# Cross-attention with a mixture-of-experts FFN on one core: when ScalarE and GpSimd split queries and single-key products, and how much of the single key's tile GpSimd splits

## The chip, the cores and the metric

The kernel runs on one core of a Trainium2 chip. The engines are TensorE (PE in the profile, with PEld for its weight loads), VectorE (DVE), ScalarE (ACT), GpSimd (POOL) and SyncE (SP), which issues the DMAs. The metric is the device time of one execution in microseconds, as the median over runs; a time is called faster or slower here when it moves by more than 0.3%.

## The reference

For each of 16 batch elements, 56 query rows of width 256 attend to 1500 context rows. The first 257 context rows (the image part) and the other 1243 (the text part) have keys, values and a softmax of their own; the two results are added.

```python
q = rms_norm(x @ q_w + q_b, nq_s).reshape(B, S, H, D)        # H = 16 heads, D = 128
k_txt = rms_norm(txt_ctx @ k_w + k_b, nkt_s).reshape(B, -1, H, D)
v_txt = (txt_ctx @ v_w + v_b).reshape(B, -1, H, D)
out_txt = sdpa(q, k_txt, v_txt)
k_img = rms_norm(img_ctx @ ki_w + ki_b, nki_s).reshape(B, -1, H, D)
v_img = (img_ctx @ vi_w + vi_b).reshape(B, -1, H, D)
out_img = sdpa(q, k_img, v_img)
out = (out_txt + out_img).reshape(B, S, INNER) @ o_w + o_b
```

A layer norm and a small mixture of 32 experts follow, with residual sums. All is in float32.

## The kernel before

The key projection is absorbed into the queries, so that attention works on the 256 columns of the context itself. The program first makes these absorbed queries (project), then runs attention over the 16 batch elements (attend), then the output projection and the experts. The change lies in attend alone.

**Tiles and steps.** The context of one batch element is cut into 13 tiles: tiles 0 to 2 are the image part, tiles 3 to 12 the text part. Tile 2 (LONE) holds one single key, since 257 = 2 x 128 + 1. All 16 heads times 56 queries are 896 columns, taken in two halves of 448. One half of one tile is a unit, so a batch element is 26 units, and every engine runs through 26 steps written out by hand. The batch loop is `batches`: its first and last passes are apart, with 14 loop passes between. Each engine executes its own list of instructions in order and waits on semaphores.

**High and low parts.** A float32 product is made of three fp32r matmuls (`three`, L1162 to L1164) of a high part and a low part of each operand. ScalarE makes a high part by a copy into fp32r (`copy`, L1314), and GpSimd or VectorE subtracts it from the original, which gives the low part.

**What each engine does for tile t** (column 0 to 255 of a tile's row of `stage` are the context with features on the partitions, columns 256 to 511 the natural layout):

- ScalarE: `prepare` (c_high, L1314, 512 columns); `exponentials` of each unit (L1341 and L1343), which at a tile's first half wait for key_rms of the tile; in some steps `split_u` (u_high, the high part of the next queries) and `split_lone` (the tile x_high in the trace, the high part of the single key's products).
- GpSimd, odd step: `split_tile` (c_low, L1636) and `twice` (c_twice, L1649; for LONE also lone_row, L1645) of a tile three steps or so ahead. After it, at the steps in LONE_LOW, `split_lone` (L1686, the low part of the single key's products, which the trace also names x_high). Even step: `key_root` (key_rms, L1630), and then one of scale_u (L1655), split_u (u_low, L1680) or scale_o (L1698).
- VectorE: `norm` (junk and key_ms, L1449), which reads c_twice; `split_probs` (p_low, L1424), `add` (L1477 or L1480) and `seed` (L1435), which writes the next unit's starting values to PSUM; at a few steps `split_sum` (p_sum_high L1488 and p_sum_low L1424, both from SBUF to SBUF).
- TensorE: the scores of a unit, the norm's products (L1169, L1171) at even steps, and the average of the unit two steps back (L1162 to L1164 with p_high), which waits for p_low.

`key_root` of a tile waits for `norm` of that tile, and `norm` waits for `twice` of that tile. For GpSimd the order is set by this part of `body`, and for ScalarE by the tuples tested at the end of its own:

```python
if step % 2 == 0:
    key_root(*ahead(it, step // 2 + 1))
else:
    split_tile(*ahead(it, step // 2 + PREP))
    twice(*ahead(it, step // 2 + PREP))
...
if has_next and step in LONE_LOW:
    split_lone(it + 1, LONE_LOW.index(step))
```

Of the kernel before, what the change touches and what calls it, by code (L numbers as in the profile page):

```python
# [23 lines left out]
F32 = mybir.dt.float32  # L24
F32R = mybir.dt.float32r
ACT = mybir.ActivationFunctionType
ALU = mybir.AluOpType
# [3 lines left out]
B, S, DIM = 16, 56, 256  # L31
# [14 lines left out]
LONE = IMG_TILES - 1  # L46
# [14 lines left out]
STAGE_RING, CTX_RING, TWICE_RING, U_RING = 3, 4, 2, 2  # L61
# [21 lines left out]
def slot(t, ring):  # L83

    return t % ring if t < TILES - 1 else ring
# [95 lines left out]
def build(nc, xT_in, ctx_in, lone_in, qw_in, kw_in, kwb_in, vw_in, small_in, router_in, bias_in, ffn_in, out):  # L181
    ctx = ExitStack()
    with ctx:
# [15 lines left out]
        with attn:  # L199
# [19 lines left out]
            with proj:  # L219

                x_high = sb("x_high", [P, NC, N], F32R, proj)
                x_low = sb("x_low", [P, NC, N], F32R, proj)
                bias_high = sb("bias_high", [P, BIAS_FLAT], F32R, proj)
                bias_low = sb("bias_low", [P, BIAS_FLAT], F32R, proj)
                square_w = sb("square_w", [P, H, 1 + 2 * H], F32R, proj)
                begun = prologue(nc, xT_in, kwb_in, small_in, psum, xT, ident, ones, minus_half, zeros, small, key_scale,
                                 bias_high, bias_low, v_bias, x_high, x_low, gram_high, gram_low, lin_rows, lin_pick,
                                 ones_r, square_w)
                by_head = [x[:, 0:2 * H * H].rearrange("p (h k) -> p h k", h=H) for x in (bias_high, bias_low)]
                spent = attend(nc, ctx_in, lone_in, qw_in, kw_in, psum, ident, minus_half, zeros, small, key_scale, *by_head,  # L230
                               x_high, x_low, square_w, gram_high, gram_low, lin_rows, lin_pick, ones_r, u_dram,
                               beta_dram, o_dram, u_stage, u_raw, q_rms_wide, is_safe, u_stored, begun)
# [568 lines left out]
def attend(nc, ctx_in, lone_in, qw_in, kw_in, psum, ident, minus_half, zeros, small, key_scale, bias_high, bias_low, x_high,  # L801
# [4 lines left out]
    with ctx:  # L806
# [3 lines left out]
        def sem(n):  # L810
            spent.append(nc.alloc_semaphore(name=n))
            return spent[-1]
# [4 lines left out]
        stage = sb("stage", [P, STAGE_RING + 1, 2 * DIM])  # L817
        c_high = sb("c_high", [P, CTX_RING + 1, 2 * DIM], F32R)
        c_low = sb("c_low", [P, CTX_RING + 1, 2 * DIM], F32R)
# [12 lines left out]
        ctx_high, ctx_low, stage_used = sem("ctx_high"), sem("ctx_low"), sem("stage_used")  # L832
# [64 lines left out]

        O = 0
        IMAGE, TEXT = 0, 1
        TEXT_SPLIT, IMAGE_SPLIT = (1, 3), (10, 12)  # L900
        LONE_TERMS, LONE_HIGH, LONE_LOW = (12, 14), (14, 16), (17, 19)
        TEXT_SUM_SPLIT, TEXT_SUMS, TEXT_RECIP = (1, 2), (3, 5), 10
        IMAGE_SUM_SPLIT, IMAGE_SUMS, IMAGE_RECIP = (7, 8), (9, 11), 16

# [718 lines left out]
        def _(gp):  # L1623
# [7 lines left out]
                    .then_inc(key_norm, 1)  # L1631

            def split_tile(it, t):
                k, st = slot(t, CTX_RING), slot(t, STAGE_RING)
                gp.wait_ge(ctx_high, TILES * it + t + 1)
                nc.gpsimd.tensor_tensor(c_low[:, k, :], stage[:, st, :], c_high[:, k, :].bitcast(F32), ALU.subtract)\  # L1636
                    .then_inc(ctx_low, 1)

            def twice(it, t):
                k, st, T = slot(t, CTX_RING), slot(t, STAGE_RING), TILES * it + t  # L1640
# [60 lines left out]
            def body(it, has_prev, has_next):  # L1701
                if not has_prev:
                    scale_first(TEXT, 0)
                for step in range(UNITS):
# [5 lines that stand above are left out]
                    if step == 0 and has_prev:  # L1710
                        scale_u(it, TEXT, 1)
                    if step == 0 and not has_prev:
                        scale_first(TEXT, 1)
                    if not has_prev and step in (1, 2):
                        split_lone(it, step - 1)
                    if has_next and step in LONE_LOW:
                        split_lone(it + 1, LONE_LOW.index(step))
                    if step in (2, 4):
                        split_u(it, TEXT, (step - 2) // 2)
                    if has_next and step in (8, 10):  # L1720
                        scale_u(it + 1, IMAGE, (step - 8) // 2)
                    if has_next and step in (12, 14):
                        split_u(it + 1, IMAGE, (step - 12) // 2)
                    if has_prev and step in (16, 18):
                        scale_o(it - 1, TEXT, (step - 16) // 2)
                    if step in (20, 22):
                        scale_o(it, IMAGE, (step - 20) // 2)
                    if has_next and step == 24:
                        scale_u(it + 1, TEXT, 0)
# [609 lines left out]
```

## Time and profile before

| | before |
|---|---|
| median of 3 runs | 1903.29 us (1898.18 to 1903.45) |
| profiled execution, its time | 1903.73 us |
| profiled execution, its span | 1902.0 us |
| mean granted TensorE clock | 0.971 |
| PE / DVE / ACT / POOL busy | 91% / 73% / 52% / 63% |

The span runs from the first to the last instruction of the one execution that was profiled. Attention lies from about 239 us to 1432 us in it. Busy shares are averages over the whole span; a matmul's row shows its whole duration, of which a part overlaps the next one.

### The profile page before, as it was taken

How to read it: one execution, taken by the hardware profiler on the slowest of the kernel's cores; microseconds unless marked ns; L12 is line 12 of the kernel's file. 1: busy time of each engine (PE TensorE's matmuls, PEld its weight loads, DVE VectorE, ACT ScalarE, POOL GpSimd, SP SyncE). 2: the span in 40 equal slices, each digit the busy share in tenths (PEclk: the TensorE clock that was granted, in tenths of full speed). 3: DMA queues.
4: the chain of work that ended last, by engine and by line, in shares of the span. 5: the costliest groups of instructions: out<-in, count | busy, mean ns of one | idle time of the engine just before them, and what ended most of it. 6: DMA issues, size and time to landing. Idle time of an engine off the chain costs nothing. (4 is left out here: it accounts for less than half of the span.)

```text
span 1902.0 us, 30825 instructions
## 1 busy us (share of the span) xinstructions
PE 1733.7 (91%) x8731; PEld 1541.6 (81%) x8731; DVE 1397.3 (73%) x2577; ACT 985.9 (52%) x1657; POOL 1204.3 (63%) x1053
## 2 busy tenths in 40 slices
PE   7899889999999999999999999999992998699998
PEld 6677778888889889888888898898891886588887
DVE  4444587887887887978878878879772664577776
ACT  3455455565555555655655565556552563244443
POOL 1333588878878888788788798798862231133332
PEclk9999899999999999999999999999996999799999
DMA  3366554566556465554565564564436782133332
GB/s 110 127 239 232 175 164 104 114 123 137 115 118 131 108 117 123 121 120 113 128 132 118 120 134 103 116 128 123 95 92 203 249 267 88 66 109 118 114 115 74
DMA packets 417365, 251.20 MB, mean 132 GB/s; under 512 B 350272, under 2 KB 368832, under 8 KB 415520
## 3 DMA queue, kind: packets, MB, share of 16 engines
q1 hardware_dynamic: 417312, 250.55, 51.5%
q8 instruction: 26, 0.43, 0.1%
q14 instruction: 27, 0.22, 0.0%
HBM read 187.71 MB, written 60.10 MB: 130 GB/s over the span
## 5 line engine op out<-in xcount | busy, mean ns | idle before, releaser
L1341 ACT ACTIVATE p_high<-psum,key_rms 128x448 fp32r<-128x448 f32 x384 | 244.8, 638 | 397.1 <-PE psum L1164 396.9
L1162 PE MATMUL psum<-p_high,c_high 128*128 128x448 f32 (+1 forms) x768 | 287.8, 375 | 48.2 <-DVE p_low L1424 48.2
L1424 DVE TENSOR_TENSOR p_low<-psum,p_high 128x448 fp32r<-128x448 f32 x384 | 236.3, 615 | 96.6 <-ACT psum L1343 95.7
L1162 PE MATMUL psum<-u_high,c_high 128*128 128x448 f32 x768 | 285.9, 372 | 20.2 <-DVE psum L1435 14.1
L1163 PE MATMUL psum<-u_low,c_high 128*128 128x448 f32 x768 | 282.9, 368 | 0.0
L1164 PE MATMUL psum<-u_high,c_low 128*128 128x448 f32 x768 | 281.8, 367 | 0.0
L1164 PE MATMUL psum<-p_high,c_low 128*128 128x448 f32 (+1 forms) x768 | 281.4, 366 | 0.0
L1163 PE MATMUL psum<-p_low,c_high 128*128 128x448 f32 (+1 forms) x768 | 281.0, 366 | 0.0
L1636 POOL TENSOR_TENSOR c_low<-stage,c_high 128x512 fp32r<-128x512 f32 x208 | 274.7, 1321 | 0.0
L1435 DVE COPY psum<-beta_wide 128x448 f32<-128x448 f32 x416 | 259.4, 627 | 20.3 <-DMA beta_wide<-absorbed_biases 4.5
L1630 POOL TENSOR_TENSOR key_rms<-key_ms,minus_half 128x1 f32<-128x1 f32 x209 | 119.4, 571 | 188.4 <-DVE key_ms L1449 183.4
L1343 ACT ACTIVATE psum<-psum,key_rms 128x448 f32<-128x448 f32 x384 | 232.5, 606 | 0.0
L1162 PEld LDWEIGHTS psum<-p_high,c_high 128*128 128x128 f32 (+1 forms) x768 | 144.0, 188 | 72.9 <-DVE p_low L1424 62.2
L1480 DVE TENSOR_TENSOR p_sum<-psum,p_sum 128x448 f32<-128x448 f32 (+1 forms) x320 | 196.2, 613 | 0.0
L1162 PEld LDWEIGHTS psum<-u_high,c_high 128*128 128x128 f32 x768 | 144.9, 189 | 44.8 <-DVE psum L1435 20.7
L2043 POOL TENSOR_TENSOR scaled_gate<-gated,p_wide 128x448 f32<-128x448 f32 x64 | 83.7, 1308 | 154.0 <-ACT gated L2144 150.5
L1649 POOL TENSOR_TENSOR c_twice<-stage,c_low 128x256 f32<-128x256 f32 x208 | 169.9, 817 | 16.4 <-POOL c_low L1636 2.4
L1449 DVE CUSTOM_DVE_ANT_0 junk<-psum,c_twice 128x257 bf16<-128x257 f32 x208 | 88.6, 426 | 92.2 <-POOL c_twice L1649 90.3
L1164 PEld LDWEIGHTS psum<-u_high,c_low 128*128 128x128 f32 x768 | 145.2, 189 | 12.7
L1163 PEld LDWEIGHTS psum<-u_low,c_high 128*128 128x128 f32 x768 | 145.2, 189 | 10.9
L1164 PEld LDWEIGHTS psum<-p_high,c_low 128*128 128x128 f32 (+1 forms) x768 | 144.1, 188 | 12.1
L1163 PEld LDWEIGHTS psum<-p_low,c_high 128*128 128x128 f32 (+1 forms) x768 | 144.3, 188 | 8.6
(245 smaller groups left out, 4077.9 us busy)
## 6 DMA issues: line engine op xcount, KB each, us to landing
stage<-in_ctx SPq DMA_DIRECT2D x210, 256.0 KB, 2.8
averages<-o_raw SPq DMA_DIRECT2D x64, 448.0 KB, 5.2
o_stage<-averages SPq DMA_DIRECT2D x32, 896.0 KB, 5.4
u_raw<-absorbed_queries SPq DMA_DIRECT2D x60, 448.0 KB, 5.5
absorbed_queries<-u_stage SPq DMA_DIRECT2D x14, 1792.0 KB, 6.8
beta_wide<-absorbed_biases SPq DMA_DIRECT2D x32, 448.0 KB, 5.3
recip_wide<-reciprocals SPq DMA_DIRECT2D x32, 448.0 KB, 4.1
p_wide<-probs_by_expert SPq DMA_DIRECT2D x32, 448.0 KB, 3.6
```

The costliest lines, as they stand in the source:

```text
L1162: nc.tensor.matmul(out, high, rhigh, start=start, stop=False, **kw)
L1163: nc.tensor.matmul(out, high, rlow, start=False, stop=False, **kw)
L1164: return nc.tensor.matmul(out, low, rhigh, start=False, stop=stop, **kw)
L1341: nc.scalar.activation(p_high[:, probs_slot(u), :], src, ACT.Exp, scale=key_rms[:, t:t + 1])
L1343: nc.scalar.activation(out, src, ACT.Exp, scale=key_rms[:, t:t + 1]).then_inc(exp_done, 1)
L1424: return nc.vector.tensor_tensor(out, a, b, ALU.subtract)
L1435: nc.vector.tensor_copy(psum[:, bank_of(u), 0:HALF], beta_wide[:, s, cols_of(half)])\
L1449: nc.vector.tensor_tensor_reduce(out=junk[:, :], in0=psum[:, GRAM, 0:DIM + 1], in1=c_twice[:, slot(t, TWICE_RING), :], scale=1.0 / INNER, ...
L1480: added = nc.vector.tensor_tensor(total, part, total, ALU.add)
L1630: nc.gpsimd.tensor_tensor(key_rms[:, t:t + 1], key_ms[:, t:t + 1], minus_half[:, 0:1], ALU.pow)\
L1636: nc.gpsimd.tensor_tensor(c_low[:, k, :], stage[:, st, :], c_high[:, k, :].bitcast(F32), ALU.subtract)\
L1649: nc.gpsimd.tensor_tensor(c_twice[:, slot(t, TWICE_RING), 0:DIM], stage[:, st, nat], c_low[:, k, nat].bitcast(F32), ALU.add).then_inc(stag ...
```

## The change

Three tuples of step numbers change, and `split_tile` takes a column range. The high parts of the next batch element's image queries go from steps 10 and 12 to 11 and 13 on ScalarE; the high parts of the single key's products go from steps 14 and 16 to 15 and 17; their low parts on GpSimd go from steps 17 and 19 to 18 and 20. For the single key's tile GpSimd subtracts only columns 256 to 511, the half that anything reads later.

```diff
-        TEXT_SPLIT, IMAGE_SPLIT = (1, 3), (10, 12)
-        LONE_TERMS, LONE_HIGH, LONE_LOW = (12, 14), (14, 16), (17, 19)
+        TEXT_SPLIT, IMAGE_SPLIT = (1, 3), (11, 13)
+        LONE_TERMS, LONE_HIGH, LONE_LOW = (12, 14), (15, 17), (18, 20)
...
             def split_tile(it, t):
-                k, st = slot(t, CTX_RING), slot(t, STAGE_RING)
+                k, st, cols = slot(t, CTX_RING), slot(t, STAGE_RING), slice(DIM if t == LONE else 0, 2 * DIM)
                 gp.wait_ge(ctx_high, TILES * it + t + 1)
-                nc.gpsimd.tensor_tensor(c_low[:, k, :], stage[:, st, :], c_high[:, k, :].bitcast(F32), ALU.subtract)\
-                    .then_inc(ctx_low, 1)
+                nc.gpsimd.tensor_tensor(c_low[:, k, cols], stage[:, st, cols], c_high[:, k, cols].bitcast(F32),
+                                        ALU.subtract).then_inc(ctx_low, 1)
```

GpSimd in the loop over the batch elements, steps 17 to 20, before (x_high is the low part of the single key's products, o_raw the scaling of finished averages):

```order
L1649 TENSOR_TENSOR c_twice<-stage,c_low 128x256
L1685 ISA
L1686 TENSOR_TENSOR x_high<-lone_terms,x_high 128x448
L1629 REGISTER_ALU
L1630 TENSOR_TENSOR key_rms<-key_ms,minus_half 128x1
L1695 REGISTER_ALU
L1698 TENSOR_TENSOR o_raw<-o_raw,recip_wide 128x2x448
L1636 TENSOR_TENSOR c_low<-stage,c_high 128x512
```

The same place of the changed kernel:

```order
L1649 TENSOR_TENSOR c_twice<-stage,c_low 128x256
L1629 REGISTER_ALU
L1630 TENSOR_TENSOR key_rms<-key_ms,minus_half 128x1
L1685 ISA
L1686 TENSOR_TENSOR x_high<-lone_terms,x_high 128x448
L1695 REGISTER_ALU
L1698 TENSOR_TENSOR o_raw<-o_raw,recip_wide 128x2x448
L1636 TENSOR_TENSOR c_low<-stage,c_high 128x512
```

The subtract of the single key's products stood between c_twice and key_rms and now stands between key_rms and o_raw; the same happens once more, at steps 19 and 20.

GpSimd at the start of a batch element in the loop, steps 0 to 3, of the changed kernel:

```order
L1630 TENSOR_TENSOR key_rms<-key_ms,minus_half 128x1
L1655 TENSOR_TENSOR u_raw<-u_raw,rms_batch 128x2x448
L1636 TENSOR_TENSOR c_low<-stage,c_high 128x256
L1645 TENSOR_TENSOR lone_row<-stage,zeros 128x2
L1649 TENSOR_TENSOR c_twice<-stage,c_low 128x256
L1630 TENSOR_TENSOR key_rms<-key_ms,minus_half 128x1
```

Here no row has moved; the c_low of the single key's tile had 128x512 and has 128x256.

## Rows read from the trace of the kernel before

**Rows 1.** Waits of PE and of POOL: engine, line, waited for, us in total, times, longest

```profile
PE psum L1162 <- DVE p_low L1424: 48.2, 48, 2.7
...
POOL key_rms L1630 <- DVE key_ms L1449: 183.4, 178, 2.9
```

**Rows 2.** Busy time by stretch of one batch element: window, length, then PE, PEld, DVE, ACT, POOL

```profile
612.10:645.10 33.00, 29.13 (x149) 25.24 (x148) 31.78 (x57) 21.10 (x37) 25.06 (x23) 1.00 0.58 128
645.10:689.30 44.20, 44.20 (x234) 41.06 (x234) 32.55 (x69) 24.79 (x44) 40.14 (x35) 1.00 0.60 121
```

**Rows 3.** Timeline of PE: start us, us, what [idle before it <- releaser]

```profile
620.93 0.47 PE L1162 MATMUL psum<-p_high,c_high 128*128 128x448 f32 x1 [1.43 <-DVE p_low L1424]
...
638.51 0.47 PE L1162 MATMUL psum<-p_high,c_high 128*128 128x448 f32 x1 [1.27 <-DVE p_low L1424]
...
677.52 0.37 PE L1162 MATMUL psum<-p_high,c_high 128*128 128x448 f32 x1
```

**Rows 4.** Timeline of DVE, steps 1 to 3 of a batch element, then later ones

```profile
612.08 0.62 DVE L1424 TENSOR_TENSOR p_low<-psum,p_high 128x448 fp32r<-128x448 f32 x1 [2.17 <-ACT psum L1343]
...
613.80 0.38 DVE L1488 CAST p_sum_high<-p_sum 128x448 fp32r<-128x448 f32 x1
614.22 1.19 DVE L1424 TENSOR_TENSOR p_sum_low<-p_sum,p_sum_high 128x448 fp32r<-128x448 f32 x1
615.33 0.42 DVE L1449 CUSTOM_DVE_ANT_0 junk<-psum,c_twice 128x257 bf16<-128x257 f32 x1
...
617.39 1.33 DVE L1488 CAST p_sum_high<-p_sum 128x448 fp32r<-128x448 f32 x1
...
645.11 0.42 DVE L1449 CUSTOM_DVE_ANT_0 junk<-psum,c_twice 128x257 bf16<-128x257 f32 x1
...
673.38 0.43 DVE L1449 CUSTOM_DVE_ANT_0 junk<-psum,c_twice 128x257 bf16<-128x257 f32 x1 [1.15 <-POOL c_twice L1649]
...
673.73 0.62 DVE L1424 TENSOR_TENSOR p_low<-psum,p_high 128x448 fp32r<-128x448 f32 x1
...
689.77 0.42 DVE L1449 CUSTOM_DVE_ANT_0 junk<-psum,c_twice 128x257 bf16<-128x257 f32 x1
```

**Rows 5.** Timeline of POOL, the same batch element

```profile
612.58 1.29 POOL L1636 TENSOR_TENSOR c_low<-stage,c_high 128x512 fp32r<-128x512 f32 x1
...
614.19 0.73 POOL L1649 TENSOR_TENSOR c_twice<-stage,c_low 128x256 f32<-128x256 f32 x1
...
618.42 1.43 POOL L1636 TENSOR_TENSOR c_low<-stage,c_high 128x512 fp32r<-128x512 f32 x1
...
660.93 0.74 POOL L1649 TENSOR_TENSOR c_twice<-stage,c_low 128x256 f32<-128x256 f32 x1
661.62 1.17 POOL L1686 TENSOR_TENSOR x_high<-lone_terms,x_high 128x448 fp32r<-128x448 f32 x1
662.73 0.56 POOL L1630 TENSOR_TENSOR key_rms<-key_ms,minus_half 128x1 f32<-128x1 f32 x1
663.25 2.14 POOL L1698 TENSOR_TENSOR o_raw<-o_raw,recip_wide 128x896 f32<-128x896 f32 x1
...
677.88 0.74 POOL L1649 TENSOR_TENSOR c_twice<-stage,c_low 128x256 f32<-128x256 f32 x1
679.17 0.55 POOL L1630 TENSOR_TENSOR key_rms<-key_ms,minus_half 128x1 f32<-128x1 f32 x1 [0.55 <-DVE key_ms L1449]
```

**Rows 6.** Timeline of ACT around the moved copies

```profile
636.08 0.96 ACT L1314 ACTIVATE u_high<-u_raw 128x896 fp32r<-128x896 f32 x1
636.94 0.61 ACT L1341 ACTIVATE p_high<-psum,key_rms 128x448 fp32r<-128x448 f32 x1
```

**Rows 7.** POOL and DVE where the second batch element begins

```profile
315.94 0.74 POOL L1649 TENSOR_TENSOR c_twice<-stage,c_low 128x256 f32<-128x256 f32 x1
...
314.36 0.63 DVE L1424 TENSOR_TENSOR p_low<-psum,p_high 128x448 fp32r<-128x448 f32 x1 [2.71 <-ACT psum L1343]
...
317.50 0.42 DVE L1449 CUSTOM_DVE_ANT_0 junk<-psum,c_twice 128x257 bf16<-128x257 f32 x1
```

## The prediction

> **What bounds the kernel now.** I read the waits first. In the attention stage TensorE waits mostly for VectorE's p_low, 48.2 us in 48 waits, and GpSimd waits 178 times for VectorE's norm, 183.4 us in all, although both are below 75% busy in the page [rows 1]. Then I read the timelines of one batch element, which repeats: the norm at 615.33 has its like at 689.77, so the period is 74.44 us [rows 4]. Busy time in two stretches of that period shows two regimes. From 612.1 to 645.1 VectorE is busy for 31.78 of 33.00 us and TensorE for only 29.13; from 645.1 to 689.3 TensorE is busy throughout, but GpSimd has 40.14 of 44.20 [rows 2].
>
> The missing 4 us of GpSimd in the second stretch is the thing to see. After c_twice of a tile, VectorE computes the norm, and only then can GpSimd go on with key_rms: 677.88 to 679.17 is 1.29 us, in which GpSimd sits idle for 0.55 [rows 5]. In turn VectorE waits for c_twice at 673.38, for 1.15 us [rows 4]. So in the second stretch GpSimd runs a closed chain, its own work plus a 0.55 us round trip for each tile, and nothing of TensorE enters it. It arrives at the c_twice of the single key's tile (614.19, and one period later 688.63), whose norm VectorE needs at once (615.33). From that norm VectorE is busy without a stop worth naming to the norm at 645.11, where GpSimd's chain starts again [rows 2, 4, 5]. I take this loop, VectorE for 30 us and GpSimd for 44 us, as what sets 74.44. TensorE's stalls, 1.43 us at 620.93 and 1.27 at 638.51 [rows 3], are where it waits for the loop.
>
> A second path reaches the norm at 615.33. VectorE starts p_low at 612.08 after ScalarE and so after TensorE [rows 4]. To the cast at 613.80 it takes 1.72, to p_sum_low 0.42, and p_sum_low itself needs about 0.49: it ran to 615.41, and c_twice ended at 614.92. That is 2.63 us against the 3.25 taken (612.08 to 615.33). The 0.62 us more is GpSimd's doing, so the TensorE path is only 0.62 us short of the loop.
>
> **The subtracts of the single key's products, steps 17 and 19 to 18 and 20.** Before, the subtract at 661.62 filled the round trip: key_rms at 662.73 shows no idle time, and from c_twice at 660.93 to o_raw at 663.25 it is 2.32 us [rows 5]. After, c_twice to key_rms is the bare 1.29, key_rms to the next instruction 0.52 (662.73 to 663.25), and the subtract 1.11 (661.62 to 662.73): 2.92 us. That is 0.60 more, twice in a batch element: GpSimd is 1.20 us later from step 20 on. Behind it stand all its later rows, the loads of stage that SyncE issues upon c_twice, and VectorE's norms. VectorE has been waiting at each norm, so it passes the delay on: p_low at 673.73 moves to 674.9 and ends at 675.5, still before TensorE needs it at 677.52 [rows 3, 4]. The loads are three tiles ahead, some 17 us (three thirteenths of 74.44), and hide it.
>
> **The shorter subtract of the single key's tile.** Now 1.29 us for 512 columns; the 256 columns of c_twice take 0.73 [rows 5]. I take 0.73, a saving of 0.56. Net, c_twice at 688.63 comes 0.64 later: 689.27 to 690.00. Without any other interference the norm starts at 690.03 in place of 689.77, 0.26 us later.
>
> **The interference.** The cast at 617.39 took 1.33 us where the one at 613.80 took 0.38; it ended 0.30 us after GpSimd's next instruction began at 618.42, and that one, of the same form as at 612.58, took 1.43 instead of 1.29 [rows 4, 5]. So a cast or a subtract of VectorE from SBUF to SBUF and an instruction of GpSimd exclude each other. In the changed kernel the cast comes at 613.80 + 74.44 = 688.24, and GpSimd's c_low at 687.02 + 1.20 = 688.22: a tie.
> - c_low first: the cast waits to 688.95 and ends at 689.26. Then p_sum_low (0.49) and c_twice (0.73) follow one another, in whichever order, to about 690.52; the norm starts at 690.55, 0.78 later than before.
> - The cast first: it is through at 688.55, c_low is pushed by 0.14 to end at 689.09, p_sum_low takes until 689.58, c_twice until about 690.25, and the norm starts at 690.28, 0.51 later.
>
> The middle, 0.65 us, is my value. The row at 617.39 speaks for the second (a waiting VectorE gets in before GpSimd's next), the 0.02 us of the tie for the first.
>
> The Trainium skill ("SBUF — State Buffer", Who interferes with whom) gives the rule behind this: VectorE's second port pair is GpSimd's only one, and whoever issues first has it for the whole instruction. The trace agrees in the 1.33 us cast; by that rule taken strictly, c_low would win the tie and the time would be 14 x 0.78 - 0.5 = 10.4 us over before, 1914.1, instead of the middle.
>
> **The moved copies of ScalarE.** I cost them at nothing. u_high at 636.08 delays the exponentials behind it, at 636.94, by up to 0.86 us [rows 6], but VectorE, which is to read them, is behind there: it is busy for 31.78 of 33.00 us. At most the 1.2 us that it idles in that stretch could be a gain, 15 x 1.2 = 18 us faster. Were ScalarE later than VectorE, the new place could cost as much. The copies' readers, GpSimd's subtracts, stand one step or more behind them; a late one would add to the 1.20.
>
> **The sum.** The delay counts at each start of a batch element in the loop, and the norm, the instructions after it and TensorE behind them shift alike, since all of them follow the loop. The first passage differs. There c_twice was already early, at 315.94, 1.58 us after VectorE's p_low at 314.36 (2.11 in the steady case, 612.08 to 614.19), and the norm was no earlier than 3.14 us after p_low, because the cast met c_twice [rows 7]. Batch element 0 lacks two scalings of GpSimd, so it can take the moved subtracts, and the shorter c_low then puts c_twice before the cast: up to 3.14 - 2.63 = 0.5 us gained, once. The sum is 14 x 0.65 - 0.5 = 8.6 us on the profiled execution's own 1903.73, so 1912.3; the median of the runs lies 0.44 below that execution, which gives **1912**.
>
> **The rivals.** What a measurement can tell from no change is about 0.3%, 5.7 us.
> - No interference remains at the norm: 14 x 0.26 - 0.5 = 3.1 us, about 1907. For it: c_twice moves away from its old meeting with p_sum_low. Against: the cast meets c_low instead.
> - The lateness is absorbed, because GpSimd waits somewhere for TensorE after all. Then only the shorter subtract counts, and the first passage shows what it is worth: 3.14 for 3.25, 0.11 us. 15 x 0.11 = 1.7 us faster, about 1902. Against: in the second stretch each idle time before key_rms is the bare 0.55.
> - Faster: GpSimd comes so early that VectorE meets none of its instructions before the norm, and the path by way of TensorE decides: 15 x 0.62 = 9 us, about 1894. It needs c_twice to end before the cast at 688.24, over 1.1 us earlier than now; the shorter subtract gives half of this, and the move takes more than that away. A gain of the moved copies of ScalarE would end there too.
> - Slower than forecast: the whole 1.20 us is paid, since a meeting eats the saving, or another one is lost downstream: 14 x 1.2 = 17 us, about 1920.
>
> **Chances.** Forecast (0.5 to 0.8 us a passage, 1910 to 1915) 0.60; no interference 0.16; absorbed 0.10; faster 0.07; the whole delay 0.07. Faster by over 0.3% is 0.07, slower 0.67, the two in between 0.26. The range goes from 1901, which takes in the absorbed case, to 1917.
>
> **What the changed profile would show.** A batch element of 75.1 us in place of 74.44; 0.55 us of idle time before the key_rms of steps 18 and 20, with the subtract behind it; o_raw 0.60 and then 1.20 us later against TensorE; c_low of the single key's tile at about 0.73 us; TensorE's stall that stood at 620.93 longer by as much as the period. If the period stays at 74.4 with those delays in place, the loop is not what I took it for. If the cast before the norm is short and p_sum_low too, the interference was mis-sized.

## The result and the profile after

The changed kernel takes 1910.02 us (median of 6 runs, 1909.05 to 1915.24) against 1901.92 us before (6 runs): the ratio is 1.005, with a 95% interval of 1.0034 to 1.0066. (The ratios here are worked out from all runs and are not the quotient of two medians, which would be 1.0043.) It is 8.1 us slower by the medians, at 1910 us for the forecast 1912; 8.6 us were forecast.

The page of the profiled execution, first part:

```profile
span 1907.3 us, 30825 instructions
## 1 busy us (share of the span) xinstructions
PE 1734.7 (91%) x8731; PEld 1538.3 (81%) x8731; DVE 1392.0 (73%) x2577; ACT 988.4 (52%) x1657; POOL 1197.2 (63%) x1053
```

POOL does 7 us less work than the 1204.3 us that its page had before, and the kernel is longer. The waits of the changed kernel (engine, line, waited for: us in total, times, longest):

```profile
PE psum L1162 <- DVE p_low L1424: 45.8, 48, 2.7
...
PE psum L1162 <- DVE psum L1435: 22.7, 29, 1.2
...
POOL key_rms L1630 <- DVE key_ms L1449: 199.9, 207, 2.9
```

Against [rows 1], GpSimd waits 29 times more for VectorE's norm and 16.5 us longer in all. 29 waits of 0.55 us would be 16 us. TensorE's wait for p_low is a little shorter; its wait for psum L1435, VectorE's seed, was 14.1 us in 15 waits before and is 22.7 in 29. The loss shows there, and not where I had put it: by the prediction the stall that stood at 620.93 in [rows 3] was to grow with the batch element, and in the changed kernel it is 1.32 us instead of 1.43, the same distance behind the first scores.

```profile
619.74 0.47 PE L1162 MATMUL psum<-p_high,c_high 128*128 128x448 f32 x1 [1.32 <-DVE p_low L1424]
```

The timeline of POOL in the changed kernel, around the first moved subtract and at the single key's tile:

```profile
659.70 0.74 POOL L1649 TENSOR_TENSOR c_twice<-stage,c_low 128x256 f32<-128x256 f32 x1
660.99 0.55 POOL L1630 TENSOR_TENSOR key_rms<-key_ms,minus_half 128x1 f32<-128x1 f32 x1 [0.55 <-DVE key_ms L1449]
661.51 1.15 POOL L1686 TENSOR_TENSOR x_high<-lone_terms,x_high 128x448 fp32r<-128x448 f32 x1
662.62 2.13 POOL L1698 TENSOR_TENSOR o_raw<-o_raw,recip_wide 128x896 f32<-128x896 f32 x1
...
686.91 0.74 POOL L1636 TENSOR_TENSOR c_low<-stage,c_high 128x256 fp32r<-128x256 f32 x1
687.81 0.19 POOL L1645 TENSOR_TENSOR lone_row<-stage,zeros 128x2 f32<-128x2 f32 x1 [0.16 <-POOL c_low L1636]
687.96 0.96 POOL L1649 TENSOR_TENSOR c_twice<-stage,c_low 128x256 f32<-128x256 f32 x1
```

From c_twice to o_raw it is 2.92 us, where [rows 5] have 2.32: the 0.55 us wait before key_rms stands bare, and the subtract comes behind it. The c_low of the single key's tile takes 0.74 us instead of 1.29. The loads of stage cost nothing more: during attention ScalarE waits for one of them twice, 6.5 us in all before and 6.4 after.

The timeline of VectorE in the changed kernel, from step 22 to the start of the next batch element:

```profile
673.32 0.43 DVE L1449 CUSTOM_DVE_ANT_0 junk<-psum,c_twice 128x257 bf16<-128x257 f32 x1 [2.30 <-POOL c_twice L1649]
...
678.57 0.43 DVE L1449 CUSTOM_DVE_ANT_0 junk<-psum,c_twice 128x257 bf16<-128x257 f32 x1 [1.27 <-POOL c_twice L1649]
678.92 0.08 DVE L1449 DVE_READ_ACCUMULATOR2_ANT key_ms<- 128x1 f32 x1
678.92 0.62 DVE L1424 TENSOR_TENSOR p_low<-psum,p_high 128x448 fp32r<-128x448 f32 x1
679.46 0.61 DVE L1480 TENSOR_TENSOR p_sum<-psum,p_sum 91x448 f32<-91x448 f32 x1
680.10 0.63 DVE L1435 COPY psum<-beta_wide 128x448 f32<-128x448 f32 x1
...
686.21 0.62 DVE L1424 TENSOR_TENSOR p_low<-psum,p_high 128x448 fp32r<-128x448 f32 x1 [1.98 <-ACT psum L1343]
...
687.94 0.39 DVE L1488 CAST p_sum_high<-p_sum 128x448 fp32r<-128x448 f32 x1
688.36 1.04 DVE L1424 TENSOR_TENSOR p_sum_low<-p_sum,p_sum_high 128x448 fp32r<-128x448 f32 x1
689.32 0.42 DVE L1449 CUSTOM_DVE_ANT_0 junk<-psum,c_twice 128x257 bf16<-128x257 f32 x1
```

VectorE waits 2.30 us for c_twice where [rows 4] have 1.15. The norm at 678.57 comes late too, and behind it stand the p_low of the last unit but one and then a copy, at 680.10. This copy is the seed of the next batch element's first unit. TensorE's timeline there:

```profile
680.78 0.48 PE L1162 MATMUL psum<-u_high,c_high 128*128 128x448 f32 x1 [0.62 <-DVE psum L1435]
```

It waits for this seed before the first scores of the batch element. In the kernel before, the same seed and the same matmul were these rows of DVE and PE, 0.39 us apart (680.18 + 0.63 to 681.20):

```profile
680.18 0.63 DVE L1435 COPY psum<-beta_wide 128x448 f32<-128x448 f32 x1
...
681.20 0.37 PE L1162 MATMUL psum<-u_high,c_high 128*128 128x448 f32 x1
```

The norms of the single key's tile (VectorE, changed kernel) give the length of a batch element: 689.32 less 614.12 is 75.20 us, where [rows 4] have 74.44.

```profile
614.12 0.42 DVE L1449 CUSTOM_DVE_ANT_0 junk<-psum,c_twice 128x257 bf16<-128x257 f32 x1
```

### The profile page after: what moved, and what is told of

The parts are those of the page before. It is cut to its first block and busy times, and to the rows that moved or that the text cites. A ratio compares the mean times of both kernels' runs of the same rounds, so it can differ in the third digit from the quotient of the medians.

```text
span 1907.3 us, 30825 instructions
## 1 busy us (share of the span) xinstructions
PE 1734.7 (91%) x8731; PEld 1538.3 (81%) x8731; DVE 1392.0 (73%) x2577; ACT 988.4 (52%) x1657; POOL 1197.2 (63%) x1053
## 5 line engine op out<-in xcount | busy, mean ns | idle before, releaser
L1162 PE MATMUL psum<-u_high,c_high 128*128 128x448 f32 x768 | 287.0, 374 | 28.8 <-DVE psum L1435 22.7
L1435 DVE COPY psum<-beta_wide 128x448 f32<-128x448 f32 x416 | 259.3, 627 | 20.4 <-DMA beta_wide<-absorbed_biases 4.5
L1636 POOL TENSOR_TENSOR c_low<-stage,c_high 128x512 fp32r<-128x512 f32 (+1 forms) x208 | 264.8, 1273 | 0.0
```

What stands on the lines that cost most here:

```text
L1162: nc.tensor.matmul(out, high, rhigh, start=start, stop=False, **kw)
L1435: nc.vector.tensor_copy(psum[:, bank_of(u), 0:HALF], beta_wide[:, s, cols_of(half)])\
L1636: nc.gpsimd.tensor_tensor(c_low[:, k, cols], stage[:, st, cols], c_high[:, k, cols].bitcast(F32), ALU.subtract).then_inc(ctx_low, 1)
```

## The experiments

The table has three numbers of each kernel's timeline besides its time. *Stall* is what TensorE loses at the first scores of a batch element: the time from the start of the matmul before them to the start of their first one, less the 0.20 us that it is without a stall. *Norm* is how long after VectorE's first p_low of a batch element the norm of the single key's tile starts (in [rows 4] 612.08 and 615.33). *Element* is the mean length of batch elements 2 to 15 (the first is 1), from first scores to first scores. Stall and norm are those of most batch elements.

| kernel | ratio to before, 95% interval | stall | norm | element |
|---|---|---|---|---|
| before | | 0 | 3.25 | 74.46 |
| changed | 1.005 (1.0034 to 1.0066) | 0.77 | 3.11 | 75.18 |
| e1, GpSimd's move only | 1.0115 (1.0099 to 1.0131) | 0.83 | 3.59 | 75.95 |
| e2, narrower c_low only | 0.9981 (0.9972 to 0.9990) | 0 | 3.11 | 74.32 |
| e3, ScalarE's moves only | 1.0000 (0.9991 to 1.0009) | 0 | 3.25 | 74.52 |
| e4, all but GpSimd's move | 0.9983 (0.9973 to 0.9993) | 0 | 3.11 | 74.29 |
| e5, steps 19 and 21 | 0.9977 (0.9966 to 0.9987) | 0 | 3.02 | 74.25 |
| e6, steps 17 and 20 | 0.9998 (0.9990 to 1.0007) | 0.19 | 3.11 | 74.61 |
| e10, norm behind the seed | 1.0069 (1.0054 to 1.0084) | 0 | 4.16 | 75.42 |
| e9, second half at step 3 | 0.9941 (0.9923 to 0.9959) | 0 | 2.69 | 73.91 |

One sum runs through the table. A batch element is 74.46, plus the stall and some 0.1 us with which the matmuls start again behind it, plus the norm's distance less 3.25. For e6 this is 74.46 + 0.19 + 0.09 - 0.14 = 74.60, for e10 74.46 + 0.91 = 75.37, for e9 74.46 - 0.56 = 73.90. For e1 it is 75.7, and 0.2 us are left over (last section). The mean of e3 holds two elements near its start of 74.96 and 74.87 us, whose cause is open; its others are 74.41 to 74.48.

### e1 to e4: the parts by themselves

e1 is the kernel before with this edit alone:

```diff
-        LONE_TERMS, LONE_HIGH, LONE_LOW = (12, 14), (14, 16), (17, 19)
+        LONE_TERMS, LONE_HIGH, LONE_LOW = (12, 14), (14, 16), (18, 20)
```

> Only the low parts of the single key's products move, steps 17 and 19 to 18 and 20; c_low of the single key's tile keeps its 512 columns, ScalarE keeps its order. Theory 1 (the move makes GpSimd 1.20 us late; VectorE's norm at step 24 passes this to the seed of the next batch element's first unit, and TensorE stalls for about 0.77 us at its first scores; behind this the whole-width c_low also makes the norm of the single key's tile later): the stall of 0.7 to 0.8 is there, the norm comes 3.3 to 3.6 us after VectorE's p_low instead of 3.11, a batch element is 75.4 to 75.8 us, 13 to 18 us over before, ratio 1.007 to 1.010. Theory 2 (only the seed's stall counts): 75.2 us as in the changed kernel, ratio 1.005. Theory 3 (the moved copies of ScalarE are what costs): no stall, 74.4 us, ratio 1.000.

It is 1.0115, slower than any theory had it: seven of its batch elements took 76.2 us, for a reason told in the last section; the other steady ones took 75.7, within the range of theory 1. The stall is there, and the norm comes at 3.59, as theory 1 said. That the seed's stall alone counts (theory 2) is refuted. The move, taken by itself, costs more than the whole change.

e2 is the kernel before with the new `split_tile` only:

```diff
-                k, st = slot(t, CTX_RING), slot(t, STAGE_RING)
+                k, st, cols = slot(t, CTX_RING), slot(t, STAGE_RING), slice(DIM if t == LONE else 0, 2 * DIM)
...
```

> Only the narrower c_low of the single key's tile; all steps as before. Theories 1 and 2: no stall at a batch element's first scores; c_twice starts 0.56 us earlier against VectorE's p_low and meets the cast, as it did at the second batch element of the kernel before, so the norm comes 3.14 us after p_low instead of 3.25: 0.11 us a batch element, 1.7 us faster, ratio 0.999. If the loop by way of GpSimd alone set the period, the gain would be up to 0.56 x 15 = 8 us, ratio 0.996. Theory 3: ratio 1.000 or just under.

Ratio 0.9981, a little below the 0.999 expected; from the first scores of the first batch element to those of the last it is 2.4 us shorter than before, for the 1.7 expected. The timelines of DVE and POOL in e2:

```profile
606.96 0.62 DVE L1424 TENSOR_TENSOR p_low<-psum,p_high 128x448 fp32r<-128x448 f32 x1 [2.17 <-ACT psum L1343]
...
608.68 0.81 DVE L1488 CAST p_sum_high<-p_sum 128x448 fp32r<-128x448 f32 x1
609.53 0.63 DVE L1424 TENSOR_TENSOR p_sum_low<-p_sum,p_sum_high 128x448 fp32r<-128x448 f32 x1
610.07 0.42 DVE L1449 CUSTOM_DVE_ANT_0 junk<-psum,c_twice 128x257 bf16<-128x257 f32 x1
...
608.51 0.74 POOL L1649 TENSOR_TENSOR c_twice<-stage,c_low 128x256 f32<-128x256 f32 x1
```

c_twice runs from 608.51 to 609.25, and the cast, started at 608.68, takes 0.81 us instead of 0.38. The 0.56 us that GpSimd saves come down to 0.14: c_twice no longer holds up p_sum_low, it holds up the cast. This is the meeting that [rows 7] show.

e3 is the kernel before with ScalarE's moves, two tuples of two steps each:

```diff
-        TEXT_SPLIT, IMAGE_SPLIT = (1, 3), (10, 12)
-        LONE_TERMS, LONE_HIGH, LONE_LOW = (12, 14), (14, 16), (17, 19)
+        TEXT_SPLIT, IMAGE_SPLIT = (1, 3), (11, 13)
+        LONE_TERMS, LONE_HIGH, LONE_LOW = (12, 14), (15, 17), (17, 19)
```

> Only ScalarE's copies move (image queries to steps 11 and 13, high parts of the single key's products to 15 and 17); GpSimd as before. Theories 1 and 2: no effect, batch element 74.4 us, ratio 0.999 to 1.001. Theory 3: ratio 1.005, a batch element of 75.2 us.

Ratio 1.0000: nothing, and theory 3 falls.

e4 is the changed kernel with one tuple put back:

```diff
-        LONE_TERMS, LONE_HIGH, LONE_LOW = (12, 14), (15, 17), (18, 20)
+        LONE_TERMS, LONE_HIGH, LONE_LOW = (12, 14), (15, 17), (17, 19)
```

> The changed kernel with the low parts of the single key's products left at steps 17 and 19 on GpSimd: ScalarE's moves and the narrower c_low stay. Theories 1 and 2: the stall at the first scores is gone, batch element 74.3 us, ratio 0.998 to 1.000. Theory 3: ratio 1.005.

Ratio 0.9983, the same as e2 within the intervals. All that makes the changed kernel slower is GpSimd's move, and it is worth 0.67% (1.005 against 0.9983).

### e5 and e6: place or lateness, and how much

e5 and e6 are the changed kernel with (19, 21) and with (17, 20) for LONE_LOW. The edit of e5:

```diff
-        LONE_TERMS, LONE_HIGH, LONE_LOW = (12, 14), (15, 17), (18, 20)
+        LONE_TERMS, LONE_HIGH, LONE_LOW = (12, 14), (15, 17), (19, 21)
```

> The changed kernel with the low parts of the single key's products one step further on, at 19 and 21: later than in the changed kernel, but behind c_twice again, where they fill the wait for the norm. If the cost is the uncovered wait of 0.55 us (place within the pair of steps), this is as fast as with steps 17 and 19: no stall at the first scores, batch element 74.3 us, ratio 0.998. If the cost is that they come later, it is as slow as the changed kernel or slower, ratio 1.005 or more.

Although they stand still later in the program than in the changed kernel, the subtracts cost no more there than at steps 17 and 19: 0.9977 against e4's 0.9983. POOL in e5:

```profile
663.85 0.74 POOL L1649 TENSOR_TENSOR c_twice<-stage,c_low 128x256 f32<-128x256 f32 x1
664.55 1.16 POOL L1686 TENSOR_TENSOR x_high<-lone_terms,x_high 128x448 fp32r<-128x448 f32 x1
665.66 0.56 POOL L1630 TENSOR_TENSOR key_rms<-key_ms,minus_half 128x1 f32<-128x1 f32 x1
```

No idle time stands before key_rms. What counts is the place behind c_twice, where the subtract fills the wait for the norm.

> The changed kernel with only the second of the two low parts moved (steps 17 and 20): GpSimd is 0.60 us late instead of 1.20. If lateness is passed on only above the margin (0.4 us between the seed and the first scores in the kernel before), the stall at the first scores is 0.2 us, a batch element 74.6 us, ratio 1.001. If each us of lateness costs the same, half of the changed kernel's distance to e4: 74.75 us, ratio 1.0015 to 1.002.

With half of the lateness the stall is 0.19 us, a quarter of 0.77, and the element is 74.61: 0.32 over e4, where half of the changed kernel's distance would be 0.45. The delay counts from the 0.39 us margin on, as the first of the two cases had it. The time, 0.9998, is 0.12% below the 1.001 expected of it, just outside its interval.

### e10: is the seed all of it?

The changed kernel, with the norm of step 24 behind the work of the last unit but one on VectorE:

```diff
-                    if step % 2 == 0 and not norms_first:
+                    if step % 2 == 0 and not norms_first and step != UNITS - 2:
                         norm(*ahead(it, step // 2 + 1))
+                    if step == UNITS - 1:
+                        norm(*ahead(it, step // 2 + 1))
```

> The changed kernel, with VectorE's norm of step 24 moved behind the last but one unit's work, into step 25: the seed of the next batch element's first unit no longer waits for GpSimd's c_twice. The stall of 0.77 us at the first scores must go in any case. If it was the only thing that made the change slower, a batch element is 74.3 to 74.5 us, ratio 0.998 to 1.000. If GpSimd's own path to the norm of the single key's tile ties with it (my step on record), the time stays: that norm comes some 4.0 us after VectorE's p_low instead of 3.11, because GpSimd is 0.4 us later still and TensorE 0.8 earlier, and a batch element takes 75.1 to 75.4 us, ratio 1.004 to 1.006.

The stall is gone, and the kernel is no faster, but slower: 1.0069, an element of 75.42 us (75.35 without two elements of 75.9, in which the clock was halved for a while, as told in the last section). VectorE and POOL in e10:

```profile
686.75 0.63 DVE L1424 TENSOR_TENSOR p_low<-psum,p_high 128x448 fp32r<-128x448 f32 x1 [0.67 <-ACT psum L1343]
...
690.91 0.43 DVE L1449 CUSTOM_DVE_ANT_0 junk<-psum,c_twice 128x257 bf16<-128x257 f32 x1 [0.78 <-POOL c_twice L1651]
...
688.75 0.90 POOL L1638 TENSOR_TENSOR c_low<-stage,c_high 128x256 fp32r<-128x256 f32 x1
689.81 0.37 POOL L1647 TENSOR_TENSOR lone_row<-stage,zeros 128x2 f32<-128x2 f32 x1 [0.16 <-POOL c_low L1638]
690.14 0.73 POOL L1651 TENSOR_TENSOR c_twice<-stage,c_low 128x256 f32<-128x256 f32 x1
```

With the first path opened, the second is there: VectorE waits 0.78 us for the c_twice of the single key's tile, and the norm comes 4.16 us after p_low. GpSimd's lateness reaches the norm of the single key's tile on two paths, and the longer hides the shorter. How long the second is without the edit is an estimate: counted from the norm before, the last c_twice ahead of the single key's comes 0.41 us later in e10 than in the changed kernel (69.31 against 68.90), because the moved norm makes GpSimd wait. Without these 0.4 us the element would be about 75.0, against 75.18 of the changed kernel and 74.29 of e4. So with the seed's stall removed and nothing else, some 0.7 of the 0.9 us would stay. No run shows that version by itself.

### e9: a version that beats both

A place behind c_twice is free only as far as GpSimd waits there, so the best is where it waits longest. At step 4, before key_rms, it waits 1.56 us; it waits 2.5 us before that of step 8, but TensorE reads the second subtract's result in step 5. e9 keeps the first subtract at step 17 and has the second at step 3 of its own batch element:

```diff
-                    if not has_prev and step in (1, 2):
-                        split_lone(it, step - 1)
-                    if has_next and step in LONE_LOW:
-                        split_lone(it + 1, LONE_LOW.index(step))
+                    if not has_prev and step == 1:
+                        split_lone(it, 0)
+                    if step == 3:
+                        split_lone(it, 1)
+                    if has_next and step == 17:
+                        split_lone(it + 1, 0)
```

> The changed kernel with the first low part back at step 17 and the second at step 3 of its own batch element, behind c_twice, where GpSimd waits 1.5 us for VectorE anyway. GpSimd's chain is 0.51 us shorter than with steps 17 and 19 (e4), so that c_twice of the single key's tile ends about when the cast begins and meets nothing: the norm comes 2.7 us after p_low instead of 3.11, a batch element takes 73.9 us, and the whole is 14 x 0.53 + 1 = 8 us faster than before, ratio 0.996, about the most that this place can give. If TensorE has to wait for the second low part (it reads it in step 5), a stall shows at the second scores of the single key, but hides behind the stall at the scores of step 8.

It is 0.9941 of the kernel before, with the element at 73.91 as expected; 0.996 was expected of the time and lies just outside the interval. Between the first scores of the first and of the last batch element it is 9.2 us shorter, of which 1.5 lie in the first element (74.49 against 75.95), which the expectation had at 1. TensorE shows no stall at the second scores of the single key. DVE and POOL in e9:

```profile
610.53 0.62 DVE L1424 TENSOR_TENSOR p_low<-psum,p_high 128x448 fp32r<-128x448 f32 x1 [2.71 <-ACT psum L1343]
...
612.26 0.38 DVE L1488 CAST p_sum_high<-p_sum 128x448 fp32r<-128x448 f32 x1
612.68 0.63 DVE L1424 TENSOR_TENSOR p_sum_low<-p_sum,p_sum_high 128x448 fp32r<-128x448 f32 x1
613.22 0.42 DVE L1449 CUSTOM_DVE_ANT_0 junk<-psum,c_twice 128x257 bf16<-128x257 f32 x1
...
611.54 0.74 POOL L1649 TENSOR_TENSOR c_twice<-stage,c_low 128x256 f32<-128x256 f32 x1
...
618.80 1.15 POOL L1686 TENSOR_TENSOR x_high<-lone_terms,x_high 128x448 fp32r<-128x448 f32 x1
620.40 0.55 POOL L1630 TENSOR_TENSOR key_rms<-key_ms,minus_half 128x1 f32<-128x1 f32 x1 [0.44 <-DVE key_ms L1449]
```

The subtract at 618.80 leaves 0.44 us of the wait. c_twice is over at 612.28, the cast and p_sum_low take 0.38 and 0.63 us, and the norm follows p_low by 2.69 us. The norm now hangs on TensorE's path alone, which my prediction had put at 2.63.

## Why the prediction was right, and where it was not

- **The loop.** Right for the kernel before and for most of the way: GpSimd's chain through the text steps, closed by the 0.55 us round trip, and VectorE's through the image steps set the length of a batch element, and each experiment that shortened or lengthened GpSimd's chain moved the time. Its last link is another in the changed kernel. There GpSimd's chain reaches TensorE by the seed, and the norm of the single key's tile follows TensorE, ScalarE and p_low; VectorE waits 1.98 us for ScalarE before that p_low.
- **The move, 0.60 us each, 1.20 in all.** Right: 2.92 against 2.32 us in the rows, o_raw 0.58 us later counted from the norm of the single key's tile (662.62 - 614.12 against 663.25 - 615.33), and e5 shows that the bare wait is the cause.
- **"So it passes the delay on: p_low at 673.73 ... still before TensorE needs it."** This step failed. I looked at one p_low and not at the seeds behind the later norms. The ring has three buffers and a batch element 26 units, so the first unit of the next one follows its buffer's last by two units and not by three. Its seed had 0.39 us of margin. The stall of 0.77 us comes from there; the passage "norm, p_low, seed, first scores" was missing from my list of what GpSimd delays. The delay did reach TensorE, by 0.77 us in each batch element.
- **The interference.** The tie of cast and c_low did not happen, because TensorE's stall brought VectorE's p_low later as well: counted from the norm before, p_low comes 0.90 us later (686.21 - 614.12 against 612.08 + 74.44 - 615.33) and c_twice 0.54. The cast took 0.39 us, and the pair that met was c_twice (0.96) with p_sum_low (1.04). Instead of 3.25 + 0.65 us the norm is at 3.11, and the rest of the 0.72 us is the stall. That the sum came out right, 0.65 forecast and 0.72 measured, is in good part luck: the path that I had costed and the one that I had missed are near each other in length, as e10 shows. The mechanism "GpSimd's lateness reaches VectorE at the start of the next batch element" was right, its price by way of this norm was not what the changed kernel pays.
- **The shorter subtract.** Right: 0.74 us for the forecast 0.73. By itself the forecast was 0.11 us a batch element, in e2 it is 0.14.
- **The first passage, 0.5 us gained.** The size came out, the mechanism did not. The norm at 317.50 in [rows 7] was to come 2.63 us after p_low instead of 3.14. In the changed kernel it comes after 3.02, since c_twice still meets the cast, which takes 0.72 us (rows below); with GpSimd's move left out, in e2 and e4, it is 2.69. The first batch element is 0.45 us shorter all the same (75.95 to 75.50), because its own norm of the single key's tile comes 0.55 us earlier after the first scores (9.02 against 9.57), and that passage I had not counted. This too is luck. DVE and POOL in the changed kernel, second batch element:

```profile
310.26 0.62 DVE L1424 TENSOR_TENSOR p_low<-psum,p_high 128x448 fp32r<-128x448 f32 x1 [2.27 <-ACT psum L1343]
...
311.99 0.72 DVE L1488 CAST p_sum_high<-p_sum 128x448 fp32r<-128x448 f32 x1
...
313.28 0.42 DVE L1449 CUSTOM_DVE_ANT_0 junk<-psum,c_twice 128x257 bf16<-128x257 f32 x1
...
311.72 0.73 POOL L1649 TENSOR_TENSOR c_twice<-stage,c_low 128x256 f32<-128x256 f32 x1
```

- **ScalarE's moves at nothing.** Right (e3).
- **The sum.** 14 x 0.72 - 0.45 = 9.6 us in the loop, against 8.6 forecast and 8.1 between the medians. The stages around the loop differ by some us from one profile to another: the first scores start at 233.1 us before and at 229.4 in the changed kernel, in stages that the change does not touch. So 1 us of difference to the medians says nothing. Small slips in the prediction's own working change nothing in it: a cast of 0.38 us is counted as 0.31, the two cases of the interference end 0.04 and 0.06 us off their own terms, and the 1914.1 has not had the 0.44 us taken off that the 1912 has.
- Open is whether port sharing alone makes the cast and GpSimd's instructions exclude each other. The rows agree with it (a cast is 0.38 us alone and 0.81 beside c_twice). The Trainium skill ("SBUF — State Buffer", Who interferes with whom) says the same of a cast that uses both of VectorE's port pairs, and of a subtract with two SBUF inputs beside a GpSimd instruction that reads SBUF. Whether this cast uses both no run shows, and none took the shared access away.

## What to carry to other kernels

When two engines hand work back and forth, look for the bare round trip (here 0.55 us before key_rms, at most text tiles) and put independent work into it; there the subtract added 0.51 us to GpSimd's chain, and one place further on its full 1.11. When an engine is made later, follow every product of its readers to the next ring wrap, since the ring's step there may be shorter than elsewhere. And before calling one stall the cost, open it: a second path of nearly the same length may stand behind it.

## What the runs showed of the hardware

e1 lost about 0.25 us a batch element more than its stalls explain. In seven of its batch elements TensorE ran for 3.4 us at a granted clock of half (1.2 instead of 2.4 GHz). Windows of e1 (length, then PE, PEld, DVE, ACT, POOL busy, granted clock, DMA share, GB/s):

```profile
697.00:702.40 5.40, 3.73 (x20) 3.07 (x18) 5.33 (x9) 3.85 (x8) 4.90 (x4) 1.00 0.91 185
702.50:706.20 3.70, 3.68 (x10) 3.29 (x11) 3.54 (x8) 0.41 (x1) 2.14 (x3) 0.54 0.22 71
706.20:712.00 5.80, 5.80 (x31) 5.08 (x31) 4.63 (x10) 3.73 (x8) 4.56 (x5) 1.00 0.14 46
```

The matmul that starts this stretch in e1:

```profile
702.52 0.61 PE L1162 MATMUL psum<-p_high,c_high 128*128 128x448 f32 x1 [1.79 <-DVE p_low L1424]
```

It takes 0.61 us, where the one at the same place takes 0.47 in [rows 3]. TensorE had been busy for 3.73 of 5.40 us before, with one idle time of 1.79. In the other kernels but e10 this idle time is 0.9 to 1.6 us, once 1.74 in e3, and the granted clock stays at 2.4 GHz from the second batch element on through the loop. In e1 it is 1.74 to 1.80 us in 14 batch elements, of which seven have such a stretch; in e10 it is 2.0 us in 15, of which two have one. So a stall of TensorE can cost more than its length: here a batch element with such a stretch took 76.2 us instead of 75.7. Which of the stalls brings the clock down, and why in one batch element and not in the next, these runs do not tell.
